# A four-layer graph network on one core: the first layer's aggregation products move into the loop that builds the adjacency

## What is computed

```
h = relu(layernorm(x));  x = x + L0(h)   # edge attention, 8 heads
h = relu(layernorm(x));  x = x + L1(h)   # sum over neighbours, W_rel and W_root
h = relu(layernorm(x));  x = x + L2(h)   # two weighted mean convolutions and a linear map
h = relu(layernorm(x));  x = x + L3(h)   # graph attention with a softmax over a node's edges
# L0: scores = (Q[src] . K[dst]) per head * sigmoid(sum(edge_attr)); out = mean over edges of V[dst]*scores, times w_o
```

## Time and profile before

| | us |
|---|---|
| median of three runs | 7470.36 (7467.83 to 7475.19) |
| the profiled execution, device time | 7471.27 |
| its span, first to last instruction | 7469.4 |

### The profile page before, as it was taken

The page is one execution under the profiler, slowest core; times in us unless marked ns, Lnnn a source line. Parts: engine busy times, 40 slices in busy tenths (PEclk is TensorE's granted clock), DMA queues, the critical chain, the costliest instruction groups (busy, mean ns, idle before and its releaser), DMA issues.

```text
span 7469.4 us, 164666 instructions
## 1 busy us (share of the span) xinstructions
PE 5787.7 (77%) x48472; PEld 4908.7 (66%) x48472; DVE 3874.9 (52%) x9331; ACT 2401.8 (32%) x7251; POOL 1834.4 (25%) x1782
## 2 busy tenths in 40 slices
PE   1777777777777779999999999999256666665665
PEld 1555555555555559999999999998244444444444
DVE  6899999999999992222111111112144444444444
ACT  2666666666666661111110000001112222222222
POOL 2000000000000000000000000000677777777771
PEclk9998988989889899999999999999577777777786
DMA  6766766667666678666667766674222222222221
GB/s 195 283 276 274 287 276 282 281 274 286 275 278 281 278 292 281 259 258 271 275 276 279 279 276 273 278 281 182 44 59 59 60 61 59 60 60 60 59 60 32
DMA packets 261005, 1542.55 MB, mean 207 GB/s; under 512 B 56235, under 2 KB 86965, under 8 KB 233836
## 3 DMA queue, kind: packets, MB, share of 16 engines
q1 hardware_dynamic: 201380, 1406.77, 48.0%
q0 software_dynamic: 59008, 129.85, 7.2%
q10 hardware_dynamic: 130, 0.80, 0.0%
HBM read 795.75 MB, written 743.08 MB: 206 GB/s over the span
## 4 chain that ended last, share of the span: by engine, by line
PE 47%; DVE 19%; POOL 13%; issue 12%; ACT 3%; ACTq 3%; DMA 2%; DVEq 0%; SPq 0%; POOLq 0%
PE psum L1113 29%; POOL field L808 12%; DVE field L1544 12%; PE psum L1078 8%; PE psum L1302 3%; PE psum L1280 3%; ACT field L921 2%; ACTq L906 2%; DVE field L1537 1%; ACT field L1009 1%; DVE field L1538 1%; DVE field L1539 1%; PE psum L1179 1%; ACTq L921 1%; DMA field<-head_table,cmp 1%
## 5 line engine op out<-in xcount | busy, mean ns | idle before, releaser
L1113 PE MATMUL psum<-field 128*128 128x128 f32 x19208 | 2255.4, 277 | 25.9 <-issue 18.8
L1113 PEld LDWEIGHTS psum<-field 128*128 128x128 f32 x19208 | 2232.5, 189 | 26.6 <-issue 19.0
L1078 PE MATMUL psum<-field 128*128 128x200 bf16 (+1 forms) x14112 | 1924.3, 281 | 132.7 <-DVE field L1544 115.6
L921 ACT COPY field<-psum x4704 | 1657.8, 416 | 959.2 <-PE psum L1078 664.4
L1544 DVE TENSOR_TENSOR field<-field 128x1176 bf16<-128x1176 bf16 x2352 | 1649.2, 761 | 0.0
L808 POOL DMA_INDIRECT field<-head_table,cmp x1563 | 1505.3, 963 | 476.3 <-issue 469.3
L1078 PEld LDWEIGHTS psum<-field 128*128 128x128 bf16 x14112 | 1077.6, 101 | 425.8 <-issue 159.0
L1069 PE MATMUL psum<-zero_b 128*128 128x2 bf16 x4704 | 807.7, 172 | 456.7 <-ACT field L921 447.9
L1069 PEld LDWEIGHTS psum<-zero_b 128*128 128x128 bf16 x4704 | 478.2, 102 | 643.5 <-issue 578.9
L752 POOL DMA_INDIRECT field<-tile_rows,step_t_i x74 | 201.0, 2716 | 2403.0 <-PE psum L1049 2355.9
L1009 ACT COPY field<-psum x1611 | 432.0, 268 | 1050.9 <-PE psum L1302 746.1
(11 more groups left out here) (288 smaller groups left out, 2572.6 us busy)
## 6 DMA issues: line engine op xcount, KB each, us to landing
adj<-field SPq DMA_DIRECT2D x882, 800.0 KB, 5.1
field<-adj SPq DMA_DIRECT2D x196, 3200.0 KB, 10.0
field<-head_table,cmp POOLq DMA_INDIRECT x1563
field<-in_edge_attr SPq DMA_DIRECT2D x4, 3072.0 KB, 25.5
head_table<-field SPq DMA_DIRECT2D x7, 476.0 KB, 3.3
tile_rows<-field SPq DMA_DIRECT2D x1, 3328.0 KB, 18.2
right_edges<-zeros SPq DMA_DIRECT2D x1, 3328.0 KB, 19.7
place_rows<-right_edges SPq DMA_DIRECT2D x25, 128.0 KB, 2.8
```

The costliest lines, as they stand in the source:

```text
L921: act.copy(evac[:, :, bass.ds(place, SEG)], build_banks[:, bass.ds(bank, NSEG * SEG)].rearrange("p (w c) -> p w c", w=NSEG)).then_inc(pair ...
L1078: mm = pe.matmul(build_banks[:, bass.ds(cur[j % ROUND], end - first)], hot, pr[:, first:end], start=False, stop=True, skip_group_check=True)
L1113: mm = pe.matmul(ps_y[slot][:, 0:D], source[:, hi, :], adj_in[slot][:, :, 2 * hi:2 * hi + 2], start=(hi == 0), stop=(hi == NB - 1))
```

## The change

In words, with the names of the new code:

- The build has 6 banks (`BUILD_BANKS`), since the seventh holds the sums of layer 0 (`ps_y0`).
- Each adjacency is kept as two arrays of 50 columns, even and odd half of the source blocks (`HALVES2`, `HALF`). A round of stores is 6 transfers in place of 3, and a block's adjacency is loaded as two halves.
- From chunk 26 on (`L0_CHUNK`), each chunk of the build also sums one block of layer 0: after each of the steps 14 to 62 of the chunk PE runs one of the 49 products of that block (`sum_part`), and ACT copies the sum to `Y` at the chunk's end (`copy_sums`). That is 47 blocks in 47 chunks; the last two blocks are summed behind the build. SP loads the halves (`load_half`), each into one buffer of its own, in the memory of X and of `work`; X is loaded again afterwards.
- The rest of layer 0 is done behind the build in 7 groups of 7 blocks (`finish`, on PE, DVE and ACT).
- The loops of PE and ACT take one chunk a round. DVE's and SP's still take two.
- `src_t` and `dst_t` are loaded by POOL behind the build, and the step rows have one buffer in place of two.

The diff, cut to its core. SP's stores and loads:

```diff
+            def load_half(b, h):
+
+                at = b * HALF_COLS + HALF
+                rows_d = adj[SIGMOID * HALVES2 + h]
+                sp.wait_ge(half_summed[h], b + HALF0)
+                sp.dma_start(half_flat[h], rows_d[:, at:at + HALF_COLS] if isinstance(b, int) else rows_d[:, bass.ds(at, HALF_COLS)])\
+                    .then_inc(half_loaded[h], 16)
...
-                        for i in range(NSEG):
-                            sp.dma_start(adj[i].rearrange("p (s c) -> p s c", c=SEG)[:, bass.ds(base[r], ROUND), :]
+                        for i in range(ARRAYS):
+                            sp.dma_start(adj[i].rearrange("p (s c) -> p s c", c=HALF)[:, bass.ds(base[r], ROUND), :]
                                          .rearrange("p s c -> p (s c)"),
-                                         evac[:, i, half * ROUND * SEG:(half + 1) * ROUND * SEG]).then_inc(pairs_stored[half], 16)
+                                         evac[:, i, half * ROUND * HALF:(half + 1) * ROUND * HALF]).then_inc(pairs_stored[half], 16)
+                        chunk, rc = k * PER_LOOP + r // (CHUNK // ROUND), r % (CHUNK // ROUND)
+                        if summing and rc == 0:
+                            load_half(chunk - L0_CHUNK, 1)
+                        if summing and rc == 2:
+                            load_half(chunk - (L0_CHUNK - 1), 0)
```

PE in the build, and behind it:

```diff
+            def sum_part(b, hi):
+
+                h, at = half_of(hi)
+                if hi == 0:
+                    pe.wait_ge(y_copied, b + DONE0)
+                    pe.sem_inc(chunk_open, 1)
+                if at == 0:
+                    pe.wait_ge(half_loaded[h], b * 16 + 16)
+                    pe.sem_inc(chunk_open, 1)
+                mm = pe.matmul(ps_y0[:, 0:D], H[:, hi, :], half_in[h][:, :, at:at + 2], start=(hi == 0), stop=(hi == NB - 1),
+                               skip_group_check=True)
+                if hi == NB - 1:
+                    for i in range(2):
+                        mm = pe.matmul(ps_y0[0:BPAIRS, D + i:D + i + 1], half_in[h][:, :, HALF - 2 + i], ones[:, 0:1], start=True, stop=True)
+                if hi == NB - 1 or half_of(hi + 1)[0] != h:
+                    mm.then_inc(half_summed[h], 1)
...
-                        pe.wait_ge(pair_copied, k * (PER_LOOP * CHUNK) + (j + 4 - BUILD_BANKS + COPIED0))
+                        pe.wait_ge(pair_copied, c * CHUNK + (j + 4 - BUILD_BANKS + COPIED0))
...
                     mm.then_inc(step_added, 1)
-                    if at == CHUNK // 2 and not (isinstance(k, int) and slot == 1):
-                        turn_step_rows(k * PER_LOOP + slot + 1, (slot + 1) % 2)
+                    if summing and Y_FIRST <= j < Y_FIRST + NB:
+                        sum_part(c - L0_CHUNK, j - Y_FIRST)
+                    if j == CHUNK // 2 and n == CHUNK:
+                        turn_step_rows(c + 1)
...
-            with pe.Fori(0, LOOPS) as k:
-                add_steps(k, PER_LOOP * CHUNK)
-            add_steps(LOOPS, TAIL_STEPS)
+            with pe.Fori(0, L0_CHUNK) as c:
+                add_steps(c, CHUNK, False)
+            pe.wait_ge(normed, GROUPS)
+            with pe.Fori(L0_CHUNK, LOOPS * PER_LOOP + 1) as c:
+                add_steps(c, CHUNK, True)
+            add_steps(LOOPS * PER_LOOP + 1, TAIL_STEPS - CHUNK, False)
```

`finish` on PE, DVE and ACT, its loops over the groups of 7 blocks:

```diff
+                for g in range(GROUPS):
+                    pe.wait_ge(fin_vs_ready, g + 1)
+                    for j in range(GROUP):
+                        mm = pe.transpose(cols(ps[0], j), cols(fin_vs, j), ident[:, :])
+                    mm.then_inc(fin_turned, 1)
+                    pe.wait_ge(fin_turn_copied, 2 * g + 2)
+                    for j in range(GROUP):
+                        mm = pe.matmul(cols(ps[1], j), cols(fin_vsT, j), W["o"], start=True, stop=True)
+                    mm.then_inc(fin_products, 1)
+                    if g + 1 < GROUPS:
+                        turn(g + 1)
+                        values(g + 1)
+                        queries(g + 1)
...
+                for g in range(GROUPS):
+                    sums(g)
+                    if g + 1 < GROUPS:
+                        scores(g + 1)
+                    scale(g)
...
+                for g in range(GROUPS):
+                    act.wait_ge(fin_turned, 2 * g + 2)
+                    act.copy(fin_vsT, ps[0][:, 0:GROUP * D]).then_inc(fin_turn_copied, 1)
+                    if g + 1 < GROUPS:
+                        turned(g + 1)
+                    act.wait_ge(block_sum, (g + 1) * GROUP)
+                    act.activation(small[:, 3, 0:GROUP], moments[:, :, 1], ACT.Sqrt, bias=epst[:, 0:1]).then_inc(block_root, GROUP)
+                    act.wait_ge(block_scaled, (g + 1) * GROUP)
...
+                    for j in range(GROUP):
+                        b = g * GROUP + j
+                        ins = act.activation(H2[:, b, :], X[:, b, :], ACT.Relu, bias=small[:, 5, j:j + 1], scale=small[:, 4, j:j + 1])
+                    ins.then_inc(block_normed, GROUP)
```

More of the change, by code:

```diff
@@ L242, in build @@
+        piece = carve(arena)
+        piece((CRING - 1) * HALVES2 * HALF_COLS)
+        src_t, dst_t, turned_t, dst_f = (piece(TCOLS3 * P) for _ in range(4))
+        fin_vsT = piece(GROUP * D)
+        piece(2 * BLOCKS)
+        place_t = turned_t
+        piece = carve(arena)
+        adj_in = [[piece(HALF_COLS) for _ in range(HALVES2)] for _ in range(CRING)]
         piece = carve(work[:, :, :].rearrange("p i f -> p (i f)"))
-        h_stage, yT, hT, vs, vsT, lin = ([piece(D) for _ in range(CRING)] for _ in range(6))
@@ L244, in build @@
-        kv = [piece(2 * D) for _ in range(CRING)]
+        h_stage, yT, hT, lin = ([piece(D) for _ in range(CRING)] for _ in range(4))
         norm_b = [small[:, i, 0:12] for i in range(CRING)]
-        head_score = [small[:, 3 + i, 0:HEADS0] for i in range(CRING)]
+        head_score = small[:, 0, 0:GROUP * HEADS0]
         piece = carve(arena)
         HT = piece(BLOCKS * ROW3).rearrange("p (b h f) -> p b h f", h=HEADS3, f=DH3 + 2)
-        piece = carve(H2flat)
-        src_t, dst_t, turned_t = (piece(TCOLS3 * P) for _ in range(3))
@@ L322, in build @@
         bases_loaded = sem("bases_loaded")
-        step_rows_landed = [sem(f"step_rows_landed{i}") for i in range(2)]
+        step_rows_landed = sem("step_rows_landed")
         chunk_open = sem("chunk_open")
@@ new lines, in copy_sums, with copy_pairs @@
+            def copy_sums(b):
+                act.wait_ge(half_summed[1], b + (1 + HALF0))
+                act.copy(one(Y, b), ps_y0).then_inc(y_copied, 1)
+            def copy_pairs(c, n, summing):
+                act.wait_ge(bank_rows_loaded, c * 16 + 16)
+                act.sem_inc(chunk_open, 1)
+                rows_of = bank_rows[0:1, c % 2, :, :, :] if isinstance(c, int) else \
+                    bank_rows[0:1, bass.ds(parity(c), 1), :, :, :].rearrange("p a q k e -> p (a q) k e")
@@ L955, in body @@
                         stage_block(0, 0)
-                    if layer == L0 and 1 <= j <= NB:
-                        act.wait_ge(kvq_ready, n)
-                        act.copy(kv[ring(layer, j, 1)], ps_kv).then_inc(kv_copied, 1)
                     if j < NB:
@@ L973, in body @@
                         stage_block(b + 1, j + 1)
-                    if layer == L0 and 1 <= j <= NB:
-                        act.wait_ge(vs_turned, n)
-                        act.copy(vsT[ring(layer, j, 1)], ps_v).then_inc(vsT_copied, 1)
                 over_blocks(act, layer, body)
-            for layer in range(4):
+            finish()
+            for layer in range(LAYERS):
                 blocks_of(layer)
-            act.wait_ge(hT_copied, 4 * NB + DONE0)
+            act.wait_ge(hT_copied, LAYERS * NB + DONE0)
             act.wait_ge(block_written, 2 * NB)
@@ L1030, in _ @@
             pe.sem_inc(y_summed, SUMMED0)
+            for h in range(HALVES2):
+                pe.sem_inc(half_summed[h], HALF0)
             pe.wait_ge(consts, CONSTS)
@@ L1225, in _ @@
+            for hi in range(NB):
+                sum_part(BLOCKS - 2, hi)
+            pe.wait_ge(y_copied, BLOCKS - 1 + DONE0)
             tables()
-            blocks_of(L0)
+            for hi in range(NB):
+                sum_part(BLOCKS - 1, hi)
+            finish()
             starts()
-            for layer in (L1, L2A, L2B):
+            for layer in range(LAYERS):
                 blocks_of(layer)
@@ L1700, in body @@
                     n = b + layer * NB
-                    if layer == L0 and 1 <= j <= NB:
-                        scores(c, n, b - 1, ring(layer, j, 1))
                     if lag <= j:
```

401 lines of the change are left out of this document (246 added, 155 removed).

## The result

The changed kernel takes 7296.32 us (7289.11 to 7305.61, four runs) against 7469.72 for the kernel before in the same rounds: a ratio of 0.9767 (95% interval 0.975 to 0.9784), 174 us less. Forecast were 7025 and a range of 6880 to 7180. What was forecast to go is gone (the pass of layer 0, ACT's stops of 6 us), but the build is some 180 us longer than forecast and layers 1 and 2 are 90 us longer than they were. Of all the executions told here one, of e12 (9495 us, at a granted clock of 0.67 where its others had 0.82 to 0.83), was in a slower state and is left out of the comparisons.

What follows compares the result with a forecast made beforehand. It took DVE as the build's bound, with ACT's stop as the rest, and PE as layer 0's. 7471.3 - 472 (layer 0) - 58 (ACT's stop) + 80 (chunks with products) = 7021, stated as 7025; range 6880 to 7180.

Steps and rivals of the forecast that it cites:

- The pass of layer 0, 666 us away, 194 in its place: Layer 0's separate pass goes, 666 us; tables, late blocks and finish behind the build cost 194, a gain of 472.
- 26 chunks without products at 33.5: In the build's first 26 chunks ACT's stop goes, gaining 2.25 us each, 58 us in all.
- six banks instead of seven leave ACT one copy less of lead; ACT's pace is below DVE's, so the wait lies under DVE's: In the build, losing one bank was claimed to cost nothing, ACT's wait being hidden under DVE's.
- the one on six stores: In the build's store rounds, six stores instead of three move the same bytes; no cost was counted.
- 47 chunks at 37.4: Build chunks with products were to take 37.4 us against 35.73, 80 us lost in all.
- 13.5 us before PE can begin step 16: At a summing chunk's start, DVE needs the split and three batches, 13.5 us from the start of PE's last batch.
- The 40 steps behind: In a summing chunk, after PE can begin step 16, 40 steps of 0.575 us were to take 23.0.
- The rival that transfers bound the chunk at 40: Transfers hold the summing chunks at 40 us: 122 us more, 7147 in all; chance 0.12.
- The rival that ACT stops every 64 steps: In the build, ACT's stop costs DVE 4.51 us twice as often as before: 7350 in all; chance 0.09.
- The rival of the half clock: In summing chunks, a late second half drops PE to half clock: 7730, or 7325 after a dozen steps; chance 0.06.
- Layers 1 to 3 "keep their products": Layers 1 to 3 keep products and order; two loads for one were to cost nothing beside PE at 0.99.
- The products were not hidden: Rival for the build: PE's waits absorb the products, every chunk runs at 33.5 to 35, 6912 at 35; chance 0.15.

Runs made afterwards that it cites:

- e12: The changed kernel as it is, on the chip of the three runs that follow: 152 us less than the kernel before, ratio 0.9819.
- e8: The kernel before with ACT's loop of the build taking one chunk a round in place of two: 7299.97 us, ratio 0.9764.
- e5: The changed kernel with products inside the build reading column pairs 96 floats apart from H, not 50 from the loaded half: 7304.6 us, ratio 0.9774.
- e9: The changed kernel with ACT's build loop begun at step 32 and the sums copied at step 4 of the next chunk: ratio 0.9711, chunk 39.4 us.
- e6: The changed kernel without the loads of halves inside the build: 7305.2 us, ratio 0.9773.
- e15: The kernel of e9 without the loads of halves, one execution: a chunk takes 39.1 us.
- e11: The changed kernel with 3 of the 49 products of a block inside the build: ratio 0.9768, chunk 40.45 us.
- e14: The changed kernel with 3 of 49 products a block and without the loads of halves, one execution: a chunk takes 35.8 us.
- e1: The kernel before with column pairs 50, 52 and 56 floats apart in layers 1, 2A and 2B: a block takes 12.43, 13.63 and 12.20 us.
- e3: The changed kernel with products of layers 1 and 2 reading column pairs 100 floats apart in place of 50: 7211.1 us, ratio 0.9653.
- e7: The changed kernel with five banks in the build in place of six: 8565.6 us, ratio 1.1464.
- e16: The kernel before with ACT's loop taking one chunk a round and beginning at step 32: 163 us less than before, ratio 0.9823.
- e17: The kernel of e9 on the chip of e16: 237 us less than the kernel before, ratio 0.9738.

## Why the prediction was wrong

- *The pass of layer 0, 666 us away, 194 in its place*: right, 202 measured. The tables and the two late blocks came out as counted, the finish's groups take 20.4 us for 19.5, and DVE waits once for X (15.5 us idle at 3049).
- *26 chunks without products at 33.5*: the mechanism was right (ACT's stop gone, 33.45 in e8), the size off by 0.7 us a chunk, 18 us. The step "six banks instead of seven leave ACT one copy less of lead; ACT's pace is below DVE's, so the wait lies under DVE's" failed, or the one on six stores beside it; which of them stays open.
- *47 chunks at 37.4*: this step failed, 40.7 measured, 47 x 3.3 = 155 us. The sum took PE and DVE as a pair ("13.5 us before PE can begin step 16") and left ACT out of it. In the chunk shown, step 16 comes 9.5 us after step 0 (2718.84 less 2709.35) and PE's last batch begins 5.5 ahead of that, 15.0 in all: PE, out of banks, stops for ACT's turn round, DVE's third batch starts 0.46 late for that, and PE loads registers at step 16. That is 1.5 of the 3.3. The 40 steps behind took 0.60 and not 0.575 each, another 1.0 (e5 shows that shorter products do count). Some 0.2 is the turn of the rows and the other register loads. The last 0.64 is the mean less this shortest chunk: in most others ACT's register load behind the jump takes up to 2.5 us in place of 1.03, and in ten the clock falls behind PE's stop. Turning ACT's loop gave back 1.3 us (e9).
- *The rival that transfers bound the chunk at 40*: not what held the changed kernel, where the loads hold 0.3 us of a chunk (e6, e15). Its number is near by luck. With few products the loads do bring the chunk to 40.4 (e11 against e14), in part by a slower clock, which the rival did not have.
- *The rival that ACT stops every 64 steps* did not come with its 4.5 us. A small part of it did: the slow register load and the clock behind it are the 0.64 us above, 30 us in 47 chunks. *The rival of the half clock* was tied to a late second half; no half was late behind the first chunk (the waits from 1077 to 2965 us name none), and its figure for a dozen slow steps, 7325, doesn't follow from its terms (12 x 0.495 x 47 = 279 gives 7304 without the stall of 3 us, 7445 with it).
- *Layers 1 to 3 "keep their products"*: this failed too, 90 us. The number of products was kept, the step between the pairs they read was not, and 11.27 / 49 = 0.23 us was the price at a step of 100 floats (e1 to e3). The products in the build read at a step of 50 too.
- The first chunk with products took 10 us more than the others: PE waited 6.3 us for its first half and then ran at half clock, which the forecast had not counted. The build began 11 us earlier, which wasn't counted either; POOL loads less ahead of it, but that this is the reason was not tried.

The sum: 18 + 155 + 10 in the build, 8 in the finish, 90 in the layers, less 11, is 270; 7025 and 270 is 7295. The products were not hidden either. Of ACT's stop, the Trainium skill says in "Runtime: NRT & Kernel Launch", "Instruction fetch mechanics", that a taken branch to a page outside the window of two pages (512 instructions for most engines, 256 a page) stalls. With 213 instructions in a round the stop is gone in e8, and with 410 it was there. That fits the rule if the round of 410 reaches into a third page, as the forecast allowed, but no run moved the place where the round of 410 starts, so this reading is not shown.

What the sum also hid is a comparison. The gain of ACT's short loop was counted beside that of the moved layer, as if one; on its own it gives all of the 174 us (e8). Against e8 the moved layer saves 666 and pays 202 behind the build, 47 x (40.7 - 33.45) = 341 and 26 x 0.75 = 20 in it, 10 in the first chunk and 90 in the layers, less the 11 of the earlier start: 652. The two kernels should then differ by 14 us; 7296 and 7300 were measured, with 10 to 17 us between the executions of each.

## What to carry to other kernels

Filling idle time of one engine in a pipeline of three pays only as long as every hand-over keeps its slack: write down, for the stage as it will be, what each engine does at the loop's start (jump, register loads, last copy) and how far the others can run ahead meanwhile, and put the jumps of coupled engines where the others are slow. When taking one suspected cost away changes nothing, look whether something else got longer with it, chunk by chunk and with the granted clock, and take two away before acquitting either. And when a change alters the layout of data, re-measure the operations that read it, even where their number and shape stay.

## What the runs showed of the hardware

- The time of a float32 matmul with 128 moving columns, taken as 64 pairs, depends on the distance between the pairs: a record (two a product) takes 272 ns at 64 and 96 floats, 275 at 2, 276 at 100, 281 at 56, 283 at 50 and 98, 298 at 52; a block of 49 products 11.5 to 13.6 us.
- ACT's stop at a jump back is 6.2 us with a round of some 410 instructions and not there with some 213 (e8). At 1439.5 us, ahead of the copy of the earlier trace rows, it has two parts: 2.4 us from the branch to the next instruction, and 3.5 us for the register load behind it, which takes 1.02 in the median. In the changed kernel that load takes 1.0 to 2.5 us in the chunks with products, and 1.0 in e8 and e9. The three numbers are ns min/median/max, before:

```profile
L906 ACTq TENSOR_LOAD <-step_words x294: 1012/1023/3527, 146.9 to 2771.3; - x147
```

- One bank fewer than six made a chunk with products 54.5 us in place of 40.7, and one without 58.2 in place of 34.2, at a granted clock of 0.85 and 0.60 in place of 0.99 (e7).
- Layer 3 took 1,600 us more in some rounds than in others for the same kernel. The record's chip 1 stands beside both (7475 us with e5 to e8, 9076 with e16 and e17), so it can't be put down to one chip or another. POOL's line of gathers is as busy as elsewhere (1,492 against 1,503 us in the changed kernel), but idle longer before it. ACT's copy of the gathered sums waits 1,484 us for what the profile calls remote, another core or a queue that it can't name; the cause is open (e12):

```profile
L871 POOL DMA_INDIRECT field<-head_table,cmp x1563 | 1491.7, 954 | 2034.8 <-PE psum L1454 1572.1
...
L1097 ACT COPY field<-psum x1611 | 433.6, 269 | 2809.3 <-remote 1483.9
```
